# Another order in the prologue of a graph-attention kernel: statistics, shared normalisation, the load of Wv and the last v projection

## The reference

```
h = jnp.maximum(_layernorm(x, axis=-1), 0.0)
q = h @ Wq.T + bq
k = h @ Wk.T + bk
v = h @ Wv.T + bv
a = q @ k.T * scale + adj + adj
attn = jax.nn.softmax(a, axis=-1)
out = x + attn @ v
```

## Time and profile before

| | before |
|---|---|
| median of 3 runs | 818.72 us (818.66, 818.72, 820.34) |
| the profiled execution | 820.26 us, of which the span of the profile is 818.5 us |
| PE busy | 806.2 us, 99% of the span |
| DVE, ACT, POOL busy | 586.9, 362.3, 384.5 us |
| DMA | 81.68 MB, mean 100 GB/s |

### The profile page before, as it was taken

How to read it: one execution, slowest core, us unless ns; L and a number is a source line. 1 busy time by engine, 2 the same in 40 slices (tenths; PEclk the granted TensorE clock), 3 DMA queues, 4 the chain that set the end, 5 groups by cost and what they waited for, 6 DMA issues and landing times.

```text
span 818.5 us, 16622 instructions
## 1 busy us (share of the span) xinstructions
PE 806.2 (99%) x6708; PEld 803.4 (98%) x6708; DVE 586.9 (72%) x978; ACT 362.3 (44%) x655; POOL 384.5 (47%) x333
## 2 busy tenths in 40 slices
PE   7899999999999999999999999999999999999998
PEld 7899999999999999999999999999999999999998
DVE  5677777776777777677777767777776777777764
ACT  4774533444443444444344444434444443444365
POOL 3453918172461717246181724617172461817263
PEclk9999999999999999999999999999999999999999
DMA  7440424323332432333243333324323332433200
GB/s 225 155 142 26 117 74 120 104 91 107 90 115 75 120 103 91 107 90 116 76 119 105 91 107 90 115 75 119 104 91 107 89 114 78 117 103 91 91 26 14
DMA packets 43997, 81.68 MB, mean 100 GB/s; under 512 B 5009, under 2 KB 5905, under 8 KB 43921
## 3 DMA queue, kind: packets, MB, share of 16 engines
q1 hardware_dynamic: 43488, 80.10, 33.2%
q10 hardware_dynamic: 432, 0.53, 0.2%
HBM read 76.42 MB, written 4.19 MB: 98 GB/s over the span
## 4 chain that ended last, share of the span: by engine, by line
PE 94%; ACT 2%; DVE 1%; POOL 1%; issue 1%; DMA 0%; SPq 0%; POOLq 0%; DVEq 0%; ACTq 0%
PE ps L332 48%; PE ps L436 15%; PE ps L434 15%; PE ps L435 15%; ACT x_pair L507 1%; PE ps L324 1%; POOL rstd L272 1%; PE ps L409 0%; DMA x_pair<-in_x 0%; PE ps L416 0%; DVE stats L597 0%; POOL v L286 0%; ACT x_third L507 0%; DVE acc L635 0%; ACT v_full L525 0%
## 5 line engine op out<-in xcount | busy, mean ns | idle before, releaser
L332 PE MATMUL ps<-qhl,hT 128*128 128x256 f32 x3072 | 406.1, 282 | 0.0
L332 PEld LDWEIGHTS ps<-qhl,hT 128*128 128x128 f32 x3072 | 383.6, 189 | 0.0
L303 POOL TENSOR_TENSOR ring_a<-ring_a,m_row 128x512 f32<-128x512 f32 x179 | 230.0, 1319 | 215.0 <-ACT m_row L576 215.0
L434 PE MATMUL ps<-v,p_hi 128*128 128x258 f32 x1024 | 291.8, 285 | 0.3 <-DVE p_lo L659 0.3
L436 PE MATMUL ps<-v,p_lo 128*128 128x258 f32 x1024 | 289.5, 283 | 0.0
L435 PE MATMUL ps<-v,p_hi 128*128 128x256 f32 x1024 | 289.1, 282 | 0.0
L572 ACT CAST p_hi<-ps 128x512 fp32r<-128x512 f32 x256 | 150.4, 587 | 245.5 <-PE ps L436 243.5
L625 DVE TENSOR_TENSOR ring_a<-ps,ring_a 128x512 f32<-128x512 f32 x179 | 123.4, 689 | 102.8 <-PE ps L332 101.8
L434 PEld LDWEIGHTS ps<-v,p_hi 128*128 128x128 f32 x1024 | 194.0, 189 | 0.5 <-DVE p_lo L659 0.5
L436 PEld LDWEIGHTS ps<-v,p_lo 128*128 128x128 f32 x1024 | 194.3, 190 | 0.0
L435 PEld LDWEIGHTS ps<-v,p_hi 128*128 128x128 f32 x1024 | 193.2, 189 | 0.0
(11 more groups left out here) (75 smaller groups left out, 360.8 us busy)
## 6 DMA issues: line engine op xcount, KB each, us to landing
ring_a<-in_adj SPq DMA_DIRECT2D x179, 256.0 KB, 2.7
ring_b<-in_adj SPq DMA_DIRECT2D x77, 256.0 KB, 2.7
x_res<-in_x SPq DMA_DIRECT2D x16, 256.0 KB, 3.0
out<-x_res SPq DMA_DIRECT2D x15, 256.0 KB, 2.0
x_pair<-in_x SPq DMA_DIRECT2D x5, 512.0 KB, 4.8
x_third<-in_x SPq DMA_DIRECT2D x2, 512.0 KB, 5.5
w_all<-in_w ACTq DMA_DIRECT2D x2, 256.0 KB, 3.9
x_pair<-in_x SPq DMA_DIRECT2D x4, 128.0 KB, 2.8
```

The costliest lines, as they stand in the source:

```text
L303: nc.gpsimd.tensor_tensor(slot_tiles(w), slot_tiles(w), m, ALU.subtract).then_inc(s_sub, 1)
L332: last = nc.tensor.matmul(dst, lhs(a, ib), rhs(c, ib), start=(n == 0), stop=(n == 3 * DB - 1))
L434: nc.tensor.matmul(ps[:, at, 0:VW], hi, v[:, n, 0:VW], start=(n == 0), stop=False)
```

## The change

- SP no longer loads Wv; ACT's queue loads it, third behind Wq and Wk and ahead of the bias columns. ACT writes Wv's high part first of all after the casts of Wq and Wk, ahead of G's high part.
- DVE makes the bias products and Wv's low part ahead of the normalisation of part 0.
- DVE takes the statistics of group 1 ahead of the low part of q for block 0.
- Parts 2 and 3 (groups 1 and 2) are normalised by DVE (tiles 0 and 1 of the group) and ACT (tiles 2 and 3) together. PE's transposition waits for both.
- PE transposes part 2 ahead of the v projection of tiles 2 and 3 of group 0.
- The last v projection (group 7, second pair) moves behind step 16's scores and uses PSUM banks 4 and 5 in place of 6 and 7; the first turn of the maximum waits for 14 of the 16 copies of v (`2 * GROUPS - 2`).

```diff
@@ PARTS
+    SPLIT_PARTS = 4
+        def v_bank(g, pair):
+            return V_BANKS[0 if g == GROUPS - 1 else pair]
@@ SP
-            sp.dma_start(w_all[:, 2 * DB * D:], w_pack[:, 2 * DB * D:WB]).then_inc(s_wv, 16)
@@ PE, transpose_h
-                if p == 0:
-                    pe.wait_ge(s_norm0, 1)
-                else:
+                if p != 1 and p < SPLIT_PARTS:
+                    pe.wait_ge(s_norm2, max(p, 1))
+                if p > 0:
                     pe.wait_ge(s_norm, p)
                     pe.wait_ge(s_hlo, p)
@@ PE, project_v and turn_max
-                    pe.wait_ge(s_vhi, 2 * (g - 1) + pair + 1)
+                    pe.wait_ge(s_vhi, 2 * g + pair if v_bank(g, pair) != V_BANKS[pair] else 2 * (g - 1) + pair + 1)
-                    pe.wait_ge(s_vhi, 2 * GROUPS)
+                    pe.wait_ge(s_vhi, 2 * GROUPS - 2)
@@ PE, the list
             scores(0)
-            pe.wait_ge(s_hlo, 2)
+            transpose_h(2)
             pe.wait_ge(s_term, 1)
             project_v(0, 1)
-            transpose_h(2)
             scores(1)
...
-                else:
+                elif g + 1 < GROUPS:
                     project_v(g, 1)
                     scores(2 * g + 1)
+            scores(FIRST - 1)
             for s in range(FIRST, STEPS + LAG + len(HOLD)):
...
+                if s == FIRST:
+                    project_v(GROUPS - 1, 1)
@@ ACT
+            nc.scalar.dma_start(w_all[:, 2 * DB * D:], w_pack[:, 2 * DB * D:WB]).then_inc(s_wv, 16)
             nc.scalar.dma_start(bias_cols[:, :], b_pack).then_inc(s_bc, 16)
...
+                if 1 < p < SPLIT_PARTS:
+                    tiles = tiles[GT // 2:]
...
+            act.wait_ge(s_wv, 16)
+            nc.scalar.copy(wv_T[:, 0, :, 0:D], wv_nat).then_inc(s_whi, 1)
             act.wait_ge(s_g, 1)
             nc.scalar.mul(G[:, 0], ...)
             h_hi(0)
-            act.wait_ge(s_wv, 16)
-            nc.scalar.copy(wv_T[:, 0, :, 0:D], wv_nat).then_inc(s_whi, 1)
@@ DVE, new function
+            def normalize(p):
+                g, tiles = part_of(p)
+                dve.wait_ge(s_rstd, p + 1)
+                for j in tiles[:GT // 2]:
+                    last = nc.vector.tensor_scalar(rows(g)[:, j], rows(g)[:, j], mean_var[:, g % XB, j, 0:1],
+                                                   rstd[:, g % XB, j:j + 1], ALU.subtract, ALU.mult)
+                last.then_inc(s_norm2, 1)
```

More of the change, by code:

```diff
@@ L154, in graph_attention_kernel @@
         s_norm = sem("x_normalized")
-        s_norm0 = sem("x_tiles_0_1_normalized")
+        s_norm2 = sem("two_x_tiles_normalized")
         s_vfull = sem("v_copied")
@@ L380, in project_v @@
                 if g > 0:
-                    pe.wait_ge(s_vhi, 2 * (g - 1) + pair + 1)
+                    pe.wait_ge(s_vhi, 2 * g + pair if v_bank(g, pair) != V_BANKS[pair] else 2 * (g - 1) + pair + 1)
                 for n in range(2):
                     t = GT * g + 2 * pair + n
-                    last = split_product(ps[:, V_BANKS[pair] + n, 0:VW],
+                    last = split_product(ps[:, v_bank(g, pair) + n, 0:VW],
                                          lambda a, ib: hT[:, a, ib, t * P:(t + 1) * P],
@@ L523, in v_hi @@
                 t = GT * g + 2 * pair
-                at = ps[:, V_BANKS[pair]:V_BANKS[pair] + 2, :]
+                at = ps[:, v_bank(g, pair):v_bank(g, pair) + 2, :]
                 nc.scalar.copy(v_full[:, pair], at[:, :, 0:D])
@@ L688, in _ @@
                                         ALU.subtract).then_inc(s_nlo, 1)
[L689 to L693, removed]
+            dve.wait_ge(s_bc, 16)
+            nc.vector.tensor_tensor(bias_products[:, :], bq_col, bk_pair[:, :, 0], ALU.mult).then_inc(s_bb, 1)
+            dve.wait_ge(s_whi, 1)
+            nc.vector.tensor_tensor(wv_T[:, 1, :, 0:D], wv_nat, wv_T[:, 0, :, 0:D].bitcast(f32),
+                                    ALU.subtract).then_inc(s_wlo, 1)
+            normalize(0)
             for j in range(GT // 2, GT):
@@ L700, in _ @@
             h_lo(0)
[L701 to L705, removed]
+            for j in range(GT):
+                tile_stats(1, j)
+            part_stats(2)
             dve.wait_ge(s_uhi, 1)
@@ L709, in _ @@
             q_lo(0)
-            for j in range(GT):
-                tile_stats(1, j)
-            part_stats(2)
             h_lo(1)
+            normalize(2)
             for j in range(GT):
@@ L716, in _ @@
             part_stats(3)
+            h_lo(2)
+            normalize(3)
             add_adj(0)
-            h_lo(2)
             for j in range(GT):
```

## The result

The changed kernel took 814.14 us (median of 6 runs, 813.87 to 815.44); the kernel before, now measured in 6 runs, 819.77. The ratio is 0.9938, 95% interval 0.9927 to 0.9948. The forecast was 813.8 in a range of 812.0 to 815.4.

What follows compares the result with a forecast made beforehand. PE, busy from 80 to 810 us, bounds the kernel, so its earlier waits count: 2.52 + (3.00 - 1.0) + 0.93 - 0.5 = 4.95 us off 818.72 (6.5 off 820.26 with the clock) gives 813.8, range 812.0 to 815.4.

Steps and rivals of the forecast that it cites:

- The frame: Whole kernel: PE is dense from 80 to 810 us, so its waits ahead of that move the end one for one.
- its signs for the profile: Group 1's transposes near 16.4 without idle, group 2's near 21.2 after about 1 us, no turn wait, first normalisation about 8.1.
- Start: First normalisation on DVE: Wv's low part and bias products ahead of it cost PE 0.5 us, bounds 0.05 and 0.65.
- The lower bound, 0.15: Price of the start if the moved work just fills DVE's idle 0.61 us: about 0.15 us.
- Group 1: PE's waits ahead of group 0's second v projection and group 1's transposes, together 2.52 us, go to 0.
- Group 2: PE's wait ahead of group 2's transposes falls from 3.00 to 1.0 us, bounds 0.6 to 1.6.
- The clock: PE's clock fall behind group 2's wait is gone: 1.56 us for an execution that had it, otherwise 0.
- the levels of before: Timed runs at 820.34 and at 818.66 and 818.72 us: parted by one fall of PE's clock, 1.6 us.
- the signs of being wrong: DVE waiting for ACT's cast of Wv, clock of 0.5 in the first 30 us, or new wait between 76 and 90.
- the first rival: The clock's fall was in the median too, so the median loses 6.5 us, to 812.2; chance 0.14.
- The last v projection: Moved behind step 16, it takes PE's wait ahead of the first turn of the maximum from 0.93 us to 0.

Runs made afterwards that it cites:

- e2: The changed kernel with Wv's load, high and low part and the bias products back in their old places; 814.19 us, ratio 0.9931.
- e8: The kernel before with only the statistics of group 1 moved ahead of the low parts of Wv's bias columns and q; 817.45 us, ratio 0.9971.
- e7: The changed kernel with group 1 alone shared by DVE and ACT, group 2 normalised by ACT alone; 814.20 us, ratio 0.9937.
- e4: The changed kernel with POOL's first low part of v waiting until DVE has normalised its two tiles of group 2; 813.10 us, ratio 0.9919.
- e3: The kernel before with 26 unused transposes of the identity in PE's wait ahead of group 2's transposes; 818.59 us, ratio 0.9984.
- e10: The changed kernel with an unused 128-column transpose of the identity beside each of the 8 bias products; 814.58 us, ratio 0.9937.
- e11: The changed kernel run once more without edits; 814.24 us, ratio 0.9932.
- e1: The kernel before with only the last v projection moved behind step 16 and its banks changed; 818.09 us, ratio 0.9982.
- e6: The changed kernel with 16 unused transposes of the identity in PE's wait ahead of group 2's transposes; 814.23 us, ratio 0.9935.
- e12: The changed kernel with POOL's wait as in e4 and ACT's two tiles of group 2 ahead of its copy of v; 812.55 us, ratio 0.9914.
- e9: The changed kernel with the 8 bias-product matmuls on PE issued twice; 816.90 us, ratio 0.9965.

## Why the prediction was right, and where it was not

- **The frame held.** PE's waits ahead of 80 us carried through to the end, and the time came out of them one for one: gaps of 2.52, 1.05 and 0.93 us removed and 0.2 at the start are 4.7 us, against 4.6 measured without falls. The forecast was 4.95, and its signs for the profile held for group 1 and the turn, not for the start and group 2.
- **Start: the term was wrong, in size and sign.** I put 0.5 us on it, since "an operation of DVE with two operands in SBUF waits for POOL". It did not wait for this one:

```profile
6.33 1.04 POOL L275 TENSOR_TENSOR rstd<-var_eps,minus_half 128x2 f32<-128x2 f32 x1
6.71 0.15 DVE L706 TENSOR_TENSOR bias_products<-bias_cols 128x2 f32<-128x2 f32 x1
6.78 0.69 DVE L708 TENSOR_TENSOR wv_T<-w_all,wv_T 128x512 fp32r<-128x512 f32 x1
7.41 0.74 DVE L618 TENSOR_SCALAR x_pair<-x_pair,mean_var,rstd 128x256 f32<-128x256 f32 x2
```

  DVE's bias products and Wv's low part ran inside POOL's rstd at their usual length, and just filled DVE's idle 0.61 us (the normalisation starts at 7.41, was 7.44). The lower bound, 0.15, was nearly right, and what it leaves out is the gain: POOL's operation for the mean, 0.74 us beside Wv's low part in the earlier trace rows, is 0.19 now that Wv's low part is elsewhere. ACT's two tiles of part 1 wait for what follows it, and the first v projection comes 0.22 us forward (e2 has Wv's low part back, and with it POOL's 0.74 us and the later v projection).
- **Group 1: right.** 2.52 to 0. e8 names the cause: the place of the statistics alone does it. Sharing group 1 and PE's new order are not needed for it. They belong together, though. In the new order PE wants group 1's rows directly behind step 0, at 15.63; ACT alone would be done at about 16.1 (an estimate: it starts at 13.99, and four tiles took it 2.07 in e7), and shared, both halves are done by 15.12.
- **Group 2: the wait was mis-sized**, 1.95 and not 1.0, outside its bounds of 0.6 to 1.6. The step that failed is "DVE: ... two tiles to 20.5": I took 0.74 us from a row where POOL was idle or in tiny operations, though in POOL's list the low parts of v come directly behind the offset of group 2. e4 shows the size of it, 2.36 to 0.73 us, and returns the 0.9 us. Otherwise the chain was right: from the first v projection to group 2's transposes the prediction has 21.2 - 13.44 = 7.76 us, and e4 measured 7.76. The Trainium skill, SBUF — State Buffer, section "Who interferes with whom", lists `tensor_scalar` among the operations of VectorE that can need the port pair shared with GpSimd. By that rule the DVE row at 18.91 waits for POOL's from 18.74, and the trace agrees that it is held up (2.36 us, to 21.27, just behind POOL's 21.12). The Trainium skill ties this to a mode with two ports, and no run here shows whether these operations were in it. I had weighed a rule of this kind at the start, where the trace does not follow it, and not here.
- **Not settled: what took group 2's wait from 3.00 to 1.95.** No run isolates it. It is not the sharing of group 2 (e7). The rows point at PE's new order: ACT's high part of group 1 starts 4.0 us behind the first v projection in e7 (12.95 to 16.96), where the transposes stand ahead of the second v projection, and 5.5 in e8 (12.73 to 18.19), where they stand behind it; ACT's tiles of group 2 start 6.56 and 7.48 us behind it. But e7 also differs from e8 in the sharing of group 1, the start and `add_adj(0)`.
- **The two errors nearly cancel.** 0.7 too much cost at the start, 0.95 too little at group 2. That the total was near is partly luck, and so is the median of the result: 4 of its 6 runs had no fall, which the forecast took as the rule.
- **The clock: right about what parts the levels of before (e3), wrong in "I take the fall as gone".** 3 of 11 runs of the changed kernel still have it, and e10 and e11 show the clock at 0.5 inside the first 30 us, which was one of the signs of being wrong. And 818.72 was not what the kernel before usually takes: 36 of 45 runs have the fall, and the median of these is 820.24. The medians differ by more (5.6 and 6.0 us) than the sum of waits, because the change also makes the fall rarer. So the condition of the first rival (the fall was in the usual run before) was true, while its number, 812.2, took the 6.5 us off a run that had no fall.
- **The last v projection: right**, 0.93 forecast, 1.0 in e1.

What stays open: where the fall is in the runs of e6 and e12 that had one, since their profiles are of runs without. In the changed kernel and its variants two places are shown (behind the wait of 1.80 us, in e10 and e11; 1.5 us behind narrow matmuls, in e9, which has twice as many of them); that the single set of bias products can do it is not shown.

## What to carry to other kernels

Where one engine is busy to the end, add up its holes ahead of the dense part, start to start, and price each by what is the last to arrive; the moves that paid were the ones that put a long dependent chain (statistics, then POOL, then ACT) ahead of short work that was wanted later. When work is moved to VectorE, look at what GpSimd will be doing at that moment: its large operations can cost as much as the move saves (e7), and one wait that orders the two gave 1 us here (e4). When few runs fall in two levels, settle what parts them before taking the median as the base.

## What the runs showed of the hardware

- VectorE and GpSimd: two `tensor_scalar` operations (128 x 256, float32, in SBUF) took 2.36 us beside two of GpSimd's 128 x 512 subtractions (the changed kernel) and 0.73 us without (e4, e9). But GpSimd's power operation on 128 x 2 (1.04 us) held up neither a 0.15 nor a 0.69 us operation of VectorE with two operands in SBUF. The other way round, a GpSimd operation on 128 x 2 took 0.74 us beside such an operation of VectorE (the kernel before and e2) and 0.19 elsewhere.
- TensorE's granted clock fell to 0.50 behind 1.80 us of idle time in some runs (e10, e11) and not in others of the same kernel. In the three kernels with 2.8 us of idle time there, 36 of 45, 6 of 12 and 7 of 8 runs had a fall (before, e1, e8), and the profiles of all three have it behind that wait. It also fell with no idle time ahead of it (e9), behind 3.5 us of matmuls of one and two columns and then 1.5 us of wide ones. Against the level without a fall, the profiled runs with the fall behind that wait took 1.3 to 1.8 us more (before, e1, e8, e10, e11), e9's took 1.0 more, and the two left in e3 took 0.5 more. Filling a wait with 26 transposes nobody needs made the kernel before 1.5 us faster in the median.
